# A division without its copy, and new order tables, in a fused cross-attention and mixture-of-experts kernel

## What is computed

```python
x = x + xattn(layernorm(x), ctx)              # x: (8, 256, 512); 16 heads of 32
# q = rms_norm(h @ w_q.T + b_q, g_q);  k likewise from ctx;  v = ctx @ w_v.T + b_v
# xattn = softmax(q k^T / sqrt(32)) v @ w_o.T + b_o
x = x + ffn(layernorm(x))                     # 2048 tokens, 8 experts, top 2, H = I = 512
# logits = h @ router_weight.T + router_bias; weights: softmax of the two largest
# gate, up = h @ gate_up_proj[e] + bias; act = (clip(up) + 1) * gate * sigmoid(1.702 * gate)
# out = sum over the two experts of weight * (act @ down_proj[e] + bias)
```

## Time and profile before

| | us |
|---|---|
| median of 3 timed runs (range) | 870.98 (867.84 to 872.41) |
| the profiled execution | 861.77 |
| its span, first to last instruction | 860.0 |
| TensorE busy | 770.0 (90%) |
| VectorE busy | 667.0 (78%) |
| ScalarE busy | 431.0 (50%) |
| GpSimd busy | 371.6 (43%) |
| mean granted TensorE clock | 0.954 of full |

### The profile page before, as it was taken

One profiled execution on the slowest core, in us unless ns is written; L12 is line 12 of the kernel. 1 busy time (PEld: TensorE's weight loads), 2 busy tenths in 40 slices (PEclk: granted clock), 3 DMA queues, 4 the chain that ended last, 5 costly groups with the idle time before them and its releaser, 6 DMA issues.

```text
span 860.0 us, 15880 instructions
## 1 busy us (share of the span) xinstructions
PE 770.0 (90%) x6245; PEld 627.9 (73%) x6245; DVE 667.0 (78%) x1281; ACT 431.0 (50%) x648; POOL 371.6 (43%) x373
## 2 busy tenths in 40 slices
PE   3988999999999999976779887889999999999995
PEld 2765777777777676754468777779888888889783
DVE  5677688777887787777767878779979797987883
ACT  4434344444344443433335734647667485757652
POOL 3213126343442525233162355274745838383523
PEclk9999899999999999978688989999999999999998
DMA  8999499998979783136066467588786768878663
GB/s 291 283 306 280 131 269 259 281 272 267 280 261 282 243 211 113 37 125 234 16 226 214 173 176 216 164 279 243 206 295 230 217 243 249 255 208 286 185 172 74
DMA packets 60776, 188.22 MB, mean 219 GB/s; under 512 B 5671, under 2 KB 6055, under 8 KB 51102
## 3 DMA queue, kind: packets, MB, share of 16 engines
q0 software_dynamic: 23584, 109.35, 39.9%
q1 hardware_dynamic: 37118, 77.86, 31.6%
HBM read 104.18 MB, written 84.84 MB: 220 GB/s over the span
## 4 chain that ended last, share of the span: by engine, by line
PE 29%; issue 17%; DVE 16%; DMA 14%; POOL 12%; ACT 10%; SPq 1%; another core or an unknown queue 1%; POOLq 0%; DVEq 0%; ACTq 0%
DMA raw<-in_wga,wx 5%; POOL out L1558 4%; POOL xs L1536 4%; PE bank L604 4%; DVE el L1172 4%; PE bank L578 3%; PE bank L606 3%; PE bank L605 3%; DMA xb<-in_x 3%; PE quad L631 3%; ACT eh L1396 3%; POOL raw L1546 3%; PE bank L668 2%; PE quad L651 2%; ACT pt L1370 2%
## 5 line engine op out<-in xcount | busy, mean ns | idle before, releaser
L1172 DVE TENSOR_TENSOR el<-raw,eh 128x2048 fp32r<-128x2048 f32 x72 | 164.6, 2287 | 43.5 <-ACT eh L1396 36.1
L1396 ACT ACTIVATE eh<-raw 128x2048 fp32r<-128x2048 f32 x72 | 137.3, 1912 | 78.6 <-DMA raw<-in_wga,wx 36.7
L766 PE MATMUL quad<-xh,eh 128*128 128x256 f32 x480 | 140.2, 292 | 0.0
L767 PE MATMUL quad<-xl,eh 128*128 128x256 f32 x480 | 137.5, 287 | 0.0
L768 PE MATMUL quad<-xh,el 128*128 128x256 f32 x480 | 137.5, 287 | 0.0
L1558 POOL DMA_INDIRECT out<-ys,ti x39 | 76.4, 1958 | 51.5 <-ACT ys L1446 32.6
L766 PEld LDWEIGHTS quad<-xh,eh 128*128 128x128 f32 x480 | 93.9, 196 | 0.2
L767 PEld LDWEIGHTS quad<-xl,eh 128*128 128x128 f32 x480 | 93.8, 195 | 0.0
L768 PEld LDWEIGHTS quad<-xh,el 128*128 128x128 f32 x480 | 93.7, 195 | 0.0
L1362 ACT ACTIVATE nm<-bank 128x256 fp32r<-128x256 f32 x32 | 12.3, 383 | 146.9 <-PE bank L578 146.9
L969 DVE TENSOR_REDUCE mx<-quad 128x8 f32<-128x2048 f32 x32 | 73.2, 2288 | 8.7 <-PE quad L631 8.7
(11 more groups left out here) (259 smaller groups left out, 2007.0 us busy)
## 6 DMA issues: line engine op xcount, KB each, us to landing
hs<-wh SPq DMA_DIRECT2D x16, 2084.0 KB, 18.1
hf<-wh SPq DMA_DIRECT2D x10, 2084.0 KB
xt<-in_x SPq DMA_DIRECT2D x8, 512.0 KB, 5.2
cr<-in_ctxT SPq DMA_DIRECT2D x8, 512.0 KB
xb<-in_x SPq DMA_DIRECT2D x8, 512.0 KB
out<-xb SPq DMA_DIRECT2D x16, 256.0 KB
pt<-in_w SPq DMA_DIRECT2D x3, 1024.0 KB, 6.1
pt<-in_w SPq DMA_DIRECT2D x4, 256.0 KB, 6.4
```

Of the source, the lines that this page charges most:

```text
L766: e.matmul(o, lh, xh[p][:, c, :], start=c == 0, stop=False)
L767: e.matmul(o, lh, xl[p][:, c, :], start=False, stop=False)
L1172: e.tensor_tensor(wl[p][part][:], raw[part][:, 0:GW], wh[p][part][:].bitcast(F32), ALU.subtract).then_inc(S_(f"e_lo{part}"), 1)
L1396: e.activation(wh[p][part][:], raw[part][:, 0:GW], ACT.Copy).then_inc(S_(f"e_hi{part}"), 1)
```

## The change

The array `den` goes. The first transposition writes `rec`, the reciprocals are read from it, and the second transposition reads `r8` with an access pattern that repeats each of 8 values 32 times, into `rec`. The copy between them is gone. All entries of the order tables are new; PERIOD and GROUP stay. The diff, its tables cut to entries that the text speaks of and the lines they stand in:

```diff
 EX = {
     "S": {
-        "turn": -29, "u0": 6, "u1": 8, "act": 35, "down0": 58, "V.xl": -31, "V.gate0": -2, "V.gate1": 18,
-        "V.sl": 32, "V.w0": -25, "V.w1": -10, "V.w2": 27, "A.xh": -35, "A.sig": 12, "A.sh": 34, "A.w0": -28,
-        "A.w1": -17, "A.w2": 12, "A.sc0": 68, "G.x": -97, "G.w0": -49, "G.w1": -48, "G.w2": -13, "G.add": 52,
+        "turn": -36, "u0": 7, "u1": 7, "act": 47, "down0": 59, "V.xl": -22, "V.gate0": 15, "V.gate1": 29,
+        "V.sl": 48, "V.w0": -21, "V.w1": -12, "V.w2": 29, "A.xh": -30, "A.sig": 19, "A.sh": 47, "A.w0": -25,
+        "A.w1": -15, "A.w2": 24, "A.sc0": 62, "G.x": -65, "G.w0": -57, "G.w1": -42, "G.w2": -3, "G.add": 60,
     },
...
     "B": {
-        "V.gate1": 35, "V.gate2": 40, "V.gate3": 51, "V.act0": 36, "V.act1": 41, "V.act2": 56, "V.act3": 58,
-        "V.al0": 44, "V.al1": 57, "V.al2": 70, "V.al3": 72, "V.w0": 8, "V.w1": 11, "V.w2": 52, "A.xh": -4,
-        "A.w0": -6, "A.w1": 12, "A.w2": 49, "A.sc0": 92, "A.sc1": 96, "G.x": -66, "G.w0": -30, "G.w1": -16,
...
+        "turn": -24, "u0": 34, "u1": 44, "u2": 45, "u3": 54, "down0": 91, "down1": 94, "V.xl": 11, "V.gate0": 29,
+        "V.gate1": 30, "V.gate2": 43, "V.gate3": 52, "V.act0": 48, "V.act1": 52, "V.act2": 57, "V.act3": 60,
+        "V.al0": 56, "V.al1": 64, "V.al2": 71, "V.al3": 81, "V.w0": 26, "V.w1": 27, "V.w2": 49, "A.xh": 0,
+        "A.w0": 13, "A.w1": 23, "A.w2": 52, "A.sc0": 84, "A.sc1": 86, "G.x": -57, "G.w0": -26, "G.w1": -20,
...
     "C": {
-        "V.gate1": 70, "V.gate2": 73, "V.gate3": 86, "V.act0": 72, "V.act1": 79, "V.act2": 85, "V.act3": 89,
-        "V.al0": 80, "V.al1": 85, "V.al2": 92, "V.al3": 94, "V.w0": 31, "V.w1": 34, "V.w2": 86, "A.xh": 21,
-        "A.w0": 24, "A.w1": 37, "A.w2": 85, "A.sc0": 113, "A.sc1": 115, "G.x": -14, "G.w0": 7, "G.w1": 16,
...
+        "turn": 41, "u0": 58, "u1": 63, "u2": 65, "u3": 86, "down0": 107, "down1": 108, "V.xl": 35, "V.gate0": 56,
+        "V.gate1": 58, "V.gate2": 86, "V.gate3": 87, "V.act0": 71, "V.act1": 87, "V.act2": 97, "V.act3": 104,
+        "V.al0": 92, "V.al1": 102, "V.al2": 111, "V.al3": 117, "V.w0": 38, "V.w1": 41, "V.w2": 84, "A.xh": 27,
+        "A.w0": 34, "A.w1": 52, "A.w2": 82, "A.sc0": 117, "A.sc1": 125, "G.x": -27, "G.w0": 23, "G.w1": 25,
...
 HEAD = {
     0: {
-        "V.sl": 58, "V.w0": -79, "V.w1": -42, "V.w2": -10, "A.xh": 1, "A.sig": 27, "A.sh": 47, "A.w0": -72,
...
+        "V.sl": 55, "V.w0": -78, "V.w1": -19, "V.w2": 14, "A.xh": 0, "A.sig": 30, "A.sh": 44, "A.w0": -87,
...
     1: {
-        "V.al0": 70, "V.al1": 78, "V.al2": 79, "V.al3": 88, "V.w0": 38, "V.w1": 41, "V.w2": 107, "A.xh": 43,
-        "A.w0": 21, "A.w1": 38, "A.w2": 120, "A.sc0": 124, "A.sc1": 129, "G.x": 21, "G.w0": -65, "G.w1": 8,
-        "G.w2": -13, "G.add": 116,
...
+        "V.al0": 58, "V.al1": 71, "V.al2": 87, "V.al3": 94, "V.w0": 35, "V.w1": 42, "V.w2": 94, "A.xh": 35,
+        "A.w0": 20, "A.w1": 25, "A.w2": 103, "A.sc0": 117, "A.sc1": 121, "G.x": 9, "G.w0": -58, "G.w1": -28,
+        "G.w2": -12, "G.add": 106,
...
-        "A.ah3": 127, "A.w0": 49, "A.w1": 49, "A.w2": 126, "A.sc0": 137, "A.sc1": 144, "G.x": 62, "G.w0": 40,
-        "G.w1": 64, "G.w2": 107, "G.add": 136,
...
+        "A.ah3": 126, "A.w0": 42, "A.w1": 57, "A.w2": 120, "A.sc0": 131, "A.sc1": 141, "G.x": 36, "G.w0": 13,
+        "G.w1": 38, "G.w2": 100, "G.add": 138,
...
     3: {
-        "V.sl": 126, "V.w0": 75, "V.w1": 78, "V.w2": 146, "A.xh": 94, "A.sig": 105, "A.sh": 130, "A.w0": 82,
-        "A.w1": 82, "A.w2": 142, "A.sc0": 161, "G.x": 63, "G.w0": 68, "G.w1": 76, "G.w2": 124, "G.add": 140,
...
+        "V.sl": 143, "V.w0": 69, "V.w1": 80, "V.w2": 144, "A.xh": 76, "A.sig": 109, "A.sh": 134, "A.w0": 72,
+        "A.w1": 78, "A.w2": 132, "A.sc0": 155, "G.x": 49, "G.w0": 61, "G.w1": 64, "G.w2": 106, "G.add": 142,
     4: {
...
-        "V.act2": 146, "V.act3": 151, "V.al0": 148, "V.al1": 150, "V.al2": 150, "V.al3": 166, "V.w0": 103,
...
-        "A.ah0": 144, "A.ah1": 146, "A.ah2": 149, "A.ah3": 163, "A.w0": 104, "A.w1": 98, "A.w2": 164, "A.sc0": 188,
-        "A.sc1": 190, "G.x": 77, "G.w0": 79, "G.w1": 77, "G.w2": 138, "G.add": 189,
...
+        "V.act2": 155, "V.act3": 161, "V.al0": 156, "V.al1": 172, "V.al2": 180, "V.al3": 183, "V.w0": 105,
+        "V.w1": 113, "V.w2": 157, "A.xh": 111, "A.us0": 142, "A.us1": 148, "A.us2": 148, "A.us3": 158,
+        "A.ah0": 146, "A.ah1": 162, "A.ah2": 169, "A.ah3": 174, "A.w0": 105, "A.w1": 114, "A.w2": 151,
+        "A.sc0": 187, "A.sc1": 194, "G.x": 54, "G.w0": 80, "G.w1": 95, "G.w2": 134, "G.add": 172,
...
 AT = {
-    "x0": -6, "x1": 50, "k0": -12, "q0": 71, "k1": 117, "q1": 128, "v0": 147, "v1": 180, "hk0": 67, "hq0": 125,
-    "hk1": 152, "hq1": 179, "peak0": 186, "peak1": 247, "peak2": 286, "peak3": 338, "m0": 188, "m1": 257,
-    "m2": 317, "m3": 352, "prob0": 236, "prob1": 260, "prob2": 320, "prob3": 379, "val0": 257, "val1": 312,
-    "val2": 354, "val3": 385, "o0": 444, "o1": 456, "r0": 458, "r1": 519, "router": 557, "rank": 582,
-    "V.stats": -78, "V.hn0": -62, "V.hn1": 32, "V.xl0": 30, "V.xl1": 49, "V.nq0": 90, "V.nq1": 136, "V.lk0": 67,
-    "V.lq0": 125, "V.lk1": 144, "V.lq1": 185, "V.max0": 212, "V.max1": 237, "V.max2": 278, "V.max3": 333,
-    "V.div0": 262, "V.div1": 303, "V.div2": 350, "V.div3": 413, "V.res0": 436, "V.res1": 475, "V.row0": 451,
-    "V.row1": 492, "V.choose": 556, "V.place": 596, "V.weigh": 563, "A.xh0": 19, "A.xh1": 39, "A.sq_k0": 4,
-    "A.sq_q0": 107, "A.sq_k1": 131, "A.sq_q1": 147, "A.nk0": 23, "A.nk1": 145, "A.hk0": 65, "A.hq0": 136,
-    "A.hk1": 166, "A.hq1": 181, "A.v0": 175, "A.v1": 186, "A.m0": 192, "A.m1": 251, "A.m2": 308, "A.m3": 363,
-    "A.exp0": 222, "A.exp1": 276, "A.exp2": 333, "A.exp3": 380, "A.oh0": 260, "A.oh1": 352, "A.oh2": 370,
-    "A.oh3": 402, "A.r0": 452, "A.r1": 511, "A.gap": 579, "G.xroot": -60, "G.root_k0": 36, "G.root_q0": 82,
-    "G.root_k1": 106, "G.root_q1": 127, "G.ol0": 260, "G.ol1": 313, "G.ol2": 368, "G.ol3": 425, "G.root2_0": 442,
-    "G.root2_1": 497, "S.load": -140, "S.resid": 405, "S.out0": 456, "S.out1": 465, "S.blank": -122, "A.ctx0": -21,
-    "G.ctx0": -52, "A.ctx1": -16, "G.ctx1": -18, "G.slots0": 579, "G.first0": 640, "G.slots1": 652,
-    "G.first1": 616, "S.blankf": 292, "V.tiles0": 610, "V.tiles1": 618, "V.tiles2": 626, "V.tiles3": 631,
-    "V.sum0": 236, "V.sum1": 277, "V.sum2": 329, "V.sum3": 374,
+    "x0": 8, "x1": 48, "k0": -6, "q0": 89, "k1": 104, "q1": 135, "v0": 140, "v1": 180, "hk0": 86, "hq0": 134,
+    "hk1": 145, "hq1": 167, "peak0": 190, "peak1": 230, "peak2": 302, "peak3": 339, "m0": 206, "m1": 260,
+    "m2": 322, "m3": 353, "prob0": 223, "prob1": 285, "prob2": 331, "prob3": 376, "val0": 241, "val1": 303,
+    "val2": 364, "val3": 383, "o0": 424, "o1": 452, "r0": 468, "r1": 525, "router": 569, "rank": 580,
+    "V.stats": -80, "V.hn0": 2, "V.hn1": 14, "V.xl0": 29, "V.xl1": 42, "V.nq0": 98, "V.nq1": 137, "V.lk0": 85,
+    "V.lq0": 136, "V.lk1": 141, "V.lq1": 185, "V.max0": 203, "V.max1": 238, "V.max2": 262, "V.max3": 336,
+    "V.div0": 253, "V.div1": 301, "V.div2": 347, "V.div3": 412, "V.res0": 437, "V.res1": 454, "V.row0": 448,
+    "V.row1": 491, "V.choose": 552, "V.place": 594, "V.weigh": 566, "A.xh0": 9, "A.xh1": 29, "A.sq_k0": -4,
+    "A.sq_q0": 84, "A.sq_k1": 100, "A.sq_q1": 151, "A.nk0": 27, "A.nk1": 147, "A.hk0": 63, "A.hq0": 137,
+    "A.hk1": 156, "A.hq1": 178, "A.v0": 162, "A.v1": 194, "A.m0": 195, "A.m1": 229, "A.m2": 290, "A.m3": 362,
+    "A.exp0": 212, "A.exp1": 275, "A.exp2": 295, "A.exp3": 380, "A.oh0": 276, "A.oh1": 328, "A.oh2": 371,
+    "A.oh3": 397, "A.r0": 444, "A.r1": 493, "A.gap": 578, "G.xroot": -97, "G.root_k0": -7, "G.root_q0": 55,
+    "G.root_k1": 90, "G.root_q1": 98, "G.ol0": 292, "G.ol1": 344, "G.ol2": 368, "G.ol3": 403, "G.root2_0": 437,
+    "G.root2_1": 473, "S.load": -234, "S.resid": 272, "S.out0": 418, "S.out1": 560, "S.blank": -16, "A.ctx0": -44,
+    "G.ctx0": -91, "A.ctx1": -17, "G.ctx1": 18, "G.slots0": 520, "G.first0": 604, "G.slots1": 653, "G.first1": 530,
+    "S.blankf": 299, "V.tiles0": 619, "V.tiles1": 629, "V.tiles2": 650, "V.tiles3": 656, "V.sum0": 233,
+    "V.sum1": 255, "V.sum2": 320, "V.sum3": 372,
 }
 
 END = {
-    "G.ol3": 385, "r0": 458, "r1": 499, "A.r0": 445, "A.r1": 517, "V.row0": 446, "V.res0": 443, "V.res1": 458,
-    "G.root2_0": 406, "G.root2_1": 473, "V.row1": 489, "router": 499, "V.choose": 524, "A.gap": 527,
-    "V.weigh": 527, "rank": 542, "V.place": 556, "S.out0": 430, "S.out1": 477, "G.slots0": 548, "G.first0": 427,
-    "G.slots1": 589, "G.first1": 488,
+    "G.ol3": 382, "r0": 462, "r1": 479, "A.r0": 476, "A.r1": 486, "V.row0": 465, "V.res0": 420, "V.res1": 442,
+    "G.root2_0": 430, "G.root2_1": 455, "V.row1": 481, "router": 491, "V.choose": 519, "A.gap": 526,
+    "V.weigh": 540, "rank": 531, "V.place": 539, "S.out0": 459, "S.out1": 535, "G.slots0": 564, "G.first0": 505,
+    "G.slots1": 549, "G.first1": 373,
 }
...
 ONCE = {
```

(17 more changed lines are left out.)

## The result

The changed kernel takes 833.89 us in the median of four runs (833.34 to 834.69), the kernel before 869.41 (867.83 to 872.41): a ratio of 0.9588, 95% interval 0.9556 to 0.9621. The prediction was 862.2 us with a range down to 853. Its direction was right and its size four times too small. On another chip the same two kernels took 836.78 and 859.86 us (ratio 0.9724, 0.9683 to 0.9765).

The account below looks back on a forecast made before the run. TensorE was taken to set the pace, 90% busy. Terms -1.8 (boundaries), -0.9 (residual), -6.7 (hand-over), 0 (expert period), +0.6 (tail) sum to -8.8 us: 853.0 profiled, 862.2 median with 9.2 added; range 853 to 876.

Parts of the forecast that it names:

- -1.8: Batch boundaries: removed copy and small waits against scatters ahead of ol1, -0.3 us each at six boundaries, range -4.5 to +4.2.
- 0.9: Attention batches: the residual's load issued a period earlier on SyncE saves 0.9 us once, bounds 0 to -1.0.
- B: Expert period gets longer, TensorE waiting in every third tile as ScalarE's w1 stands behind sh: 877 us; chance 0.14.
- D: Division: the spread transposition costs as much as copy and transposition together, 7 x 0.4 us: 865 us; chance 0.05.
- Rival C: Batch boundaries: scatters ahead of ol1 cost 0.7 us at five, +3.5 in place of -1.8: 867.5 us; chance 0.10.
- 0.6 of its pieces: Hand-over from attention to experts: pieces sum to -11.1 us, 6 parts in 10 counted, -6.7, between all and rival A.
- the tail +0.6: Kernel's end: act.T23 moves behind down1.T22, which hid it, adding 0.6 us.
- The wait at 413: Hand-over: TensorE's 2.71 us wait for maxima; moving w1 of tile 0 behind max3 was to save 2.3 us.
- the one at 497: Hand-over: TensorE's 6.75 us wait for tile 1's down weights; slots 5.8 us earlier were to save 5.8 us.
- The first edit: Hand-over: V.w1 of tile 0 goes from 1699 to 1743, behind the last batch's max3; -2.3 us, 0 to -2.5.
- G.w2: Hand-over, third edit: G.w2 of tile 3 moves before add.T1 against TensorE's last two waits; -3 us, 0 to -5.
- The 7.24 us wait: Hand-over: TensorE's wait for an exponential, ended by nothing named, 4.75 us marked remote; costed at nothing, bounds -5 and +3.

Follow-up runs that it names:

- e13: Changed kernel with G.slots0 back at 579, the first half's scatters behind ol1 and ol2 of the next batch: 837.27 us, changed kernel on the same chip 836.78.
- e10: Changed kernel with the place of batch 7's slots (V.place, rank) back at its old step on VectorE: 838.73 us.
- e8: Changed kernel with the low half of w1 of tile 0 on VectorE back ahead of the third key sum and last maxima: 838.57 us.
- e14: Changed kernel with GpSimd's entries (input, three weight loads, addition) of tiles 0 to 5 old: 866.81 us, 1.0084 of before.
- e2: Kernel before with the new division alone, all tables old: 871.37 us, ratio 0.9968 to before.
- e4: Kernel before with the new order of the last batch's end and new weight-step places of tiles 0 to 5: 900.91 us, 1.0311 of before.
- e5: Kernel before with G.ctx1 alone moved from -18 to 41, behind the scatters: 865.09 us, 0.9958 of before.
- e9: Kernel before with G.ctx1 at 41 and SyncE's entries from the new table: 855.93 us, 0.9964 of before.
- e6: Changed kernel with G.ctx1 put back to -18, ahead of root_k0, ol3 and first0: 869.84 us, 1.0061 of before.
- e3: Kernel before with four attention entries new (A.ctx0, A.ctx1, G.ctx0, G.ctx1): 902.51 us, 1.031 of before.
- e15: Changed kernel as it is, on another chip: 836.78 us, where before took 859.86.
- e1: The change without its last hunk, so all new tables with the old division: 834.41 us, ratio 0.9525 to before.
- e12: Changed kernel with the 24 first_tiles address instructions moved behind max0 of batch 7: 839.44 us.
- e16: Changed kernel with first_tiles behind division 3 of batch 6, G.w0 of tile 0 behind first0, A.w0 behind the exponential: 839.05 us.

## Why the prediction was wrong

**Right.** The copy is gone at no measurable time. The spread transposition costs 446 ns, as taken. Batches of 46.5 to 46.8 us against a forecast of 46.8, six batches -2.5 us against -1.8 - 0.9. Expert periods of 49.08 us, inside 48.5 to 49.5. Rivals B and D did not come: no period of 51 us, no dear transposition. Rival C came in part: VectorE's product does wait some 2 us for ol at five boundaries, but TensorE does not, and with the scatters back behind ol (e13), where that wait is gone, the time is the same.

```profile
183.26 0.42 DVE L988 TENSOR_TENSOR of<-bank,rec 128x256 f32<-128x256 f32 x1 [1.97 <-POOL ol L1578]
```

**What failed, in short.** The sum stopped at -8.8 us where the traces show -28.2: it put nothing on the first batch (-5.8), cut the hand-over to 0.6 of its pieces (-6.7, and -10.8 came), and gave the tail +0.6 (-2.4 came). The largest remaining piece, -6.1 around the wait that it costed at nothing, may not be the change's. Then it put the kernel before's 9.2 us between profiled run and median on the changed kernel too, where they are 0.3.

**The factor of 0.6.** The pieces of the hand-over summed to -11.1 us and 10.8 came. I took 6 parts in 10 for fear that the gain would land in the next wait. But it came by other ways than my pieces. The wait at 413 fell by 0.23 us to 2.48, not by 2.3, and the one at 497 to 3.39, where I had both under 1. The slots are written 3.5 us behind the ranks (455.89 to 459.40) where it was 12.0, so 8.5 us sooner and not 5.8, but that place undone alone (e10) costs 2.1 to 2.5 us by the traces and 4.7 by the medians. The first edit undone alone (e8) costs the 2.3 us that I had put on it. And G.w2, costed at -3, stands in a group whose old form costs 30 (e14). That the whole is near 11 us is luck; of its steps only the first is borne out at its price.

**Stretches left out.** I read the earlier trace rows from 192 us on and took the first batch for settled: -5.8 us. The 7.24 us wait I costed at 0 with a bound of -5, since nothing named ended it; it fell by 5.3 and its stretch by 6.1 between these two traces, but other runs of both sets of tables have it short or long, so the 0 is not refuted. In the tail I summed TensorE's steps (+0.6) and not the additions behind its last product, which gave -2.4. With 4.1 from the factor, 0.6 from the experts and 0.2 too much for the batches that makes 5.8 + 6.1 + 3.0 + 4.1 + 0.6 - 0.2 = 19.4, which is 28.2 less 8.8.

**The step from the profiled run to the median.** I added 9.2 us to both. It belongs to before alone: the changed kernel's profiled run is 0.3 us below its median. e2, e4 and e5, which have before's order of those transfers, in e5 with one entry mended, show waits for the scatter or the residual. The profiled before had just escaped the first; GpSimd, SyncE and VectorE at the place of e2's rows:

```profile
193.51 1.00 POOL L1605 DMA_INDIRECT hf<-hr,si  x1 [0.31 <-issue]
194.67 1.01 SPq L1628 DMA_DIRECT2D cr<-in_ctxT  x1
197.90 0.55 DVE L1014 TENSOR_SCALAR hr<-xb,mvb,rsb 128x512 f32<-128x512 f32 x1
```

Here the load was issued 0.16 us behind the end of the scatter's second part, and VectorE did not wait; in e2 it was issued 1.17 us ahead of that part, and VectorE waited 3.72 us. I had called the place of G.ctx1 a matter of VectorE's company. It is what holds the load behind the scatter. That such waits make up the 7.3 us is not shown: there is no trace of a slower run of before itself, and with both of them gone e9 is 3.4 us faster in the median and spreads as before. That the changed kernel is free of the 7.3 is shown (runs within 1.4 and 2.6 us of each other on two chips), and e6 shows what it would pay without G.ctx1's new place.

## What to carry to other kernels

Ask of each transfer that an engine must wait for how far ahead of its neighbours on the DMA engines it is issued, and what enforces that order: a margin of one microsecond does not show in a single profile. Where the timed runs lie 1% above the profiled one, carry the difference over to the changed kernel only with a reason, and take a second trace: a long wait in one of two traces need not be the change's. Orders of several engines are one plan: here single parts of a plan worth 4% cost 3%, so a sum over its edits doesn't forecast it, and an entry put back alone shows what hangs on it, not its share. Read every stretch in which the clock falls, the first one too: a wait of 2.1 to 2.7 us cost another 1.7 to 3.4 in clock.

## What the runs showed of the hardware

**Clock.** Behind the first batch's wait for the key sum, the granted clock from 85 to 90 us was 0.50 to 0.74 in the four runs with a wait of 2.14 to 2.66 us (before, e2, e4, e6), and 1.00 in the thirteen others that reach it with 1.07 to 1.70; in e3 it had fallen earlier. Over 85 to 95 us it was 0.66 in before and 0.83 in the other three, 3.4 and 1.7 us lost.

**Two engines side by side.** In before, e2, e4 and e6 GpSimd's 128x512 subtraction started ahead of VectorE's 128x1024 sum, and the sum took 2.17 to 2.29 us in place of 1.23; in e3 the sum started first and kept its 1.23, and the subtraction took 2.01.

**A wait with no name.** At exponential 1 of batch 7 ScalarE stood 4.75 us in the profiled before, 4.04 in e9, and 2.9 to 3.9 in e10 to e15, with its end put down to "remote". The row of e9:

```profile
393.13 1.88 ACT L1276 ACTIVATE pt<-quad 128x2048 f32<-128x2048 f32 x1 [4.04 <-remote]
```

The semaphore that ends it is TensorE's own, raised by the last product of the logits. In before that product starts at 393.90 and the exponential at 399.50, 5.6 us behind it; in the changed kernel they start at 384.77 and 385.11, 0.3 us apart. So the semaphore, or the product's real end, came late; which, and why, the traces don't tell. The changed kernel's profiled run lacks the delay, e15, the same kernel, has it. It goes with the chip more than with the tables: none of the eight runs e1 to e8 on two chips has it, with old or new tables, all four of e9 to e12 do, and of e13 to e16 only e16, whose order ahead of it is another, does not. In before and e9 one of 25 packets of the queue q14 (instruction) landed 2.0 and 1.1 us ahead of its end, in e10 to e15 none did, and e13 has 1.6 to 2.0 us of it at the first exponential of five batches too, which is too regular for a chance; before has it at one such place as well, hidden but for 0.4 us (product 188.54, exponential 190.51). The cause stays open, and some 5 of the 28.2 us rest on it.
